# A graph network layer on one core: order of the vector steps, a third PSUM home for gathered rows, and another order at the end

## The chip, the cores and the metric

One core of one Trainium2 chip. The metric is device time of one execution in microseconds (us), median of the runs shown. Engines: TensorE (PE in the profile; PEld its weight loads), VectorE (DVE), ScalarE (ACT), GpSimd (POOL), SyncE (SP, DMA issue only).

## What is computed

Two graph layers over N = 256 nodes with 512 features and E = 4352 edges. The change lies in the second layer; cut to it, the reference is:

```python
hs = xs @ w_in2f_s / sqrt(B);  hv = einsum('nbc,bf->nfc', xv, w_in2f_v) / sqrt(B)   # B = 128, F = 32
s, v = hs[idx_j], hv[idx_j]                   # gather by edge
h = ssp(f_ij @ W1 + b1)                       # ssp(x) = softplus(x) - log 2
Wf = ((h @ W2 + b2) * rcut).reshape(-1, F, 6)
# per edge, with ys = Yr[:, 0], yv = Yr[:, 1:4]: s*ys*Wf0, (v.yv)*Wf1/sqrt 3, s*yv*Wf2, v*ys*Wf3
agg = segment_sum(edge, idx_i, n)             # scatter by edge
s_in = concat(agg[..., 0], agg[..., 1]);  v_in = concat(agg[..., 2:5], agg[..., 5:8])
os1 = ssp(s_in @ w_f2o1_s / sqrt(2F));    os2 = os1 @ w_f2o2_s / sqrt(B)
ov2 = (v_in through w_f2o1_v, then w_f2o2_v, each scaled)
out = x + concat(os2, ov2)
```

## The kernel before

Edges lie on partitions, in 34 tiles of 128, in nine groups of four tiles (the last, group 8 = `LATE`, has two). For each group, counted here by g, the engines do:

- **PE gathers** (`gather`, L721): one-hot columns times the node channels `HL`, whose high and low parts give 128x256 per tile in PSUM; the group's rows live in a pair of PSUM banks, `gpair[g % 2]`, so two groups are in flight. `gather(g)` waits for `MA` of group g - 2, the last step of VectorE that reads that pair.
- **ACT** copies the low parts out (`rows_lo`, L284, semaphore `Glo`), rounds the finished messages to `Mh` (L301 for half 1, released by `svw`; L305 for half 0, released by `MA`), and makes the scatter one-hots `OsR` of the next group (L240). Its order in the iteration of group g is L301(g), L305(g), L240(g + 1), L284(g + 2).
- **VectorE** adds high and low parts (`rows_sum`, L514, semaphore `add`), multiplies by filters times harmonics (`times_w2_y`, L534, `Q`), writes one product to the messages (`times_w1`, L529, `vys`), another (`s_w2_times_y`, L546, `svw`), reduces over three components in place (`sum_of_vy`, L540, `red`), and writes the last product (L565, `MA`). `sum_of_vy` writes over what `times_w1` reads, so it waits for `vys`, then `Q`.
- **POOL** makes the remainders `Ml` = M - Mh of both halves (L395, L399) and scales filters of a later group (L378).
- **PE scatters** (`scatter`, L733): the one-hots against `Mh` and `Ml` into two running aggregates, 0 in bank 4 and 1 in bank 5.

The last groups are scattered in pieces (`scatter_part`, L742), high and low parts apart, as they come; the remainders of group 8 and of half 0 of group 7 are made on VectorE (L572, semaphores `MlA_late`, `MlB_late`). Then aggregate 0 is copied by VectorE (L575) and aggregate 1 by ACT (L313), and two branches follow. The **scalar branch**: L782 (matmul, `os1`), ACT's Abs, Exp and Ln (L315, L317, L319), VectorE's scaled maximum with zero (L577) and the sum of both (L588), L795 (matmul), L591 and the DMA issued by ACT (L321). The **vector branch**: six matmuls (L788 to L790, `fin`), additions of x (L583, L584), and two DMAs on SP's queue (L193). Each engine runs its instructions in the order written here; semaphores are the only other order.

Of the kernel before, what the change touches and what calls it, by code (L numbers as in the profile page):

```python
# [5 lines left out]
def gnn_preln_kernel(nc, x, idx, dst_row, f_t, yr, w0, bias0, w1, w2, b2, w_in, w_o1s, w_o1vt, w_o2s, w_o2v,  # L6
# [8 lines left out]
    P = 128  # L15
# [38 lines left out]
    with ctx:  # L54
# [3 lines left out]
        def sem(name):  # L58
# [74 lines left out]
        ta, te, te2, os1T = (za[:, i * N:(i + 1) * N] for i in range(4))  # L133
# [16 lines left out]
                 "scatA aggA aggT wc wcs o1 os1 ta te tl rl os1T fin os2 ov o")  # L150
# [8 lines left out]
        gpair = (pair[0], pair[3])  # L159
# [7 lines left out]
        def rows_of(g):  # L167

            return gpair[g % 2][:, 0:tiles(g) * 2 * C].rearrange("p (t h c f) -> p t h c f", t=tiles(g), h=2, c=4)
# [27 lines left out]
        def _(act):  # L197
# [114 lines left out]
            act.wait_ge(q["scat"], NG)  # L312
            nc.scalar.activation(aggT[:, 1, :], bank[5][:, 0:N], ACT.Copy).then_inc(q["aggT"], 1)  # L313
# [91 lines left out]
        def _(dve):  # L405
# [113 lines left out]
            for g in range(NG):  # L519
# [55 lines left out]
            nc.vector.tensor_copy(aggT[:, 0, :], bank[4][:, 0:N]).then_inc(q["aggA"], 1)  # L575
            dve.wait_ge(q["ta"], 1)
            nc.vector.tensor_scalar(te2[:], bank[2][:, 0:N], SF, 0.0, ALU.mult, ALU.max).then_inc(q["rl"], 1)  # L577
            for a in range(NH):
                dve.wait_ge(q["fin"], a + 1)
                ov = o_sb[:, a, B:].rearrange("p (d c) -> p c d", c=3)  # L580
                xv = x1[:, a, B:].rearrange("p (d c) -> p c d", c=3)
                xz = bank[a][:, 0:2 * B].rearrange("p (c d) -> p c d", c=2)
                nc.vector.tensor_tensor(ov[:, 0:3:2, :], xz, xv[:, 0:3:2, :], ALU.add)  # L583
                nc.vector.tensor_tensor(ov[:, 1, :], bank[6 + a][:, 0:B], xv[:, 1, :], ALU.add).then_inc(q["ov"], 1)  # L584
                if a == 0:
                    dve.wait_ge(q["tl"], 1)
                    dve.wait_ge(q["rl"], 1)
                    nc.vector.tensor_tensor(os1T[:], te2[:], ta[:], ALU.add).then_inc(q["os1T"], 1)  # L588
# [6 lines left out]
        def _(pe):  # L595
# [109 lines left out]
            def gather(g):  # L705
# [152 lines left out]
```

## Time and profile before

| | us |
|---|---|
| median of 3 runs | 71.74 (71.64 to 71.81) |
| the profiled execution's own time | 71.83 |
| its span, first to last instruction | 69.8 |
| PE, DVE, ACT, POOL busy | 61.7, 60.1, 48.6, 39.5 |
| granted TensorE clock over the span | 0.988 of full |

The span is 2.03 us shorter than the execution's time; what lies around it is not in the trace. The loop over groups takes 34.56 to about 61 us of the span, the rest of the scatter and the two branches take the last nine.

### The profile page before, as it was taken

To read this page: it belongs to the slowest core of one execution; us is meant where nothing else is said; L and a number is where in the kernel's file an instruction comes from. 1 tells how busy PE (TensorE), PEld (TensorE's weight loads), DVE (VectorE), ACT (ScalarE), POOL (GpSimd) and SP (SyncE) were. 2 spreads that over 40 slices of the span, in tenths; PEclk is the share of its full clock that TensorE was granted. 3 is DMA by queue.
4 is the path that set the end of the run, shared out by engine and by line. 5 is a ranking of instruction groups with operands and counts; after the bars stand their busy time and mean duration, and the time that the engine had idled before them with its cause. 6 is when DMAs were issued, how large, how long until landed. Compare 5 with 4: busy or idle time off the path is not lost.

```text
span 69.8 us, 1215 instructions
## 1 busy us (share of the span) xinstructions
PE 61.7 (88%) x407; PEld 48.6 (70%) x407; DVE 60.1 (86%) x124; ACT 48.6 (70%) x74; POOL 39.5 (57%) x46
## 2 busy tenths in 40 slices
PE   3999998999999999897998979999999999998340
PEld 1236754568834268796987969998898989997220
DVE  4599999999979968989999898989898999972760
ACT  0700059978999697967979999988696969732700
POOL 5000030000676989594799979999999988700000
PEclk9999999999999999999999999999999999999995
DMA  0899998984000000000000000000000000000044
GB/s 1 129 396 247 361 499 379 449 317 124 9 0 0 0 0 0 0 0 5 0 0 0 0 0 9 5 0 0 0 0 0 0 0 9 0 0 0 0 148 153
DMA packets 3049, 5.65 MB, mean 81 GB/s; under 512 B 540, under 2 KB 1936, under 8 KB 2916
## 3 DMA queue, kind: packets, MB, share of 16 engines
q1 hardware_dynamic: 2274, 5.14, 21.3%
q10 hardware_dynamic: 770, 0.44, 2.2%
q8 instruction: 3, 0.05, 0.3%
q14 instruction: 2, 0.02, 0.1%
HBM read 5.06 MB, written 0.52 MB: 80 GB/s over the span
## 4 chain that ended last, share of the span: by engine, by line
DVE 45%; PE 20%; issue 14%; ACT 13%; DMA 3%; DVEq 0%; ACTq 0%
ACT OsR L240 8%; DVE WQ L412 7%; DVE Os L412 7%; PE pair L632 5%; ACT w_sb L284 5%; DVE dst_bc L565 4%; PE pair L733 4%; PE pair L742 4%; DVE pair L514 3%; PE pair L674 3%; DMA idx_sb<-idx 3%; PE pair L721 3%; DVE w_sb L485 2%; DVE za L446 2%; DVE hX L449 2%
## 5 line engine op out<-in xcount | busy, mean ns | idle before, releaser
L733 PE MATMUL pair<-OsR,Mh 128*128 128x256 f32 x56 | 13.6, 281 | 0.0
L733 PE MATMUL pair<-OsR,Ml 128*128 128x256 f32 x56 | 13.6, 281 | 0.0
L721 PE MATMUL pair<-HL,OdT 128*128 128x256 f32 x68 | 10.1, 289 | 1.6 <-DVE dst_bc L565 0.7
L395 POOL TENSOR_TENSOR Ml<-dst_bc,Mh 128x512 fp32r<-128x512 f32 x8 | 10.4, 1305 | 1.1 <-ACT Mh L301 1.0
L721 PEld LDWEIGHTS pair<-HL,OdT 128*128 128x128 f32 x68 | 8.6, 188 | 2.8 <-issue 2.8
L733 PEld LDWEIGHTS pair<-OsR,Ml 128*128 128x128 f32 x56 | 10.5, 188 | 0.0
L733 PEld LDWEIGHTS pair<-OsR,Mh 128*128 128x128 f32 x56 | 10.5, 188 | 0.0
L605 PEld LDWEIGHTS pair<-WQ,Os 128*128 128x128 bf16 x68 | 6.8, 104 | 4.0 <-DVE WQ L412 1.8
L605 PE MATMUL pair<-WQ,Os 128*128 128x256 bf16 x68 | 9.4, 297 | 0.2 <-DVE WQ L412 0.2
L399 POOL TENSOR_TENSOR Ml<-dst_bc,Mh 128x512 fp32r<-128x512 f32 x7 | 9.2, 1309 | 0.0
L240 ACT ACTIVATE OsR<-Os 128x1024 fp32r<-128x1024 bf16 (+1 forms) x9 | 9.0, 999 | 0.0
L632 PE MATMUL pair<-w_sb,h1T 128*128 128x512 f32 x16 | 7.7, 601 | 0.3 <-ACT h1T L214 0.3
L305 ACT ACTIVATE Mh<-dst_bc 128x512 fp32r<-128x512 f32 (+1 forms) x9 | 5.5, 609 | 3.1 <-DVE dst_bc L565 3.0
L514 DVE TENSOR_TENSOR pair<-pair,w_sb 128x512 f32<-128x512 f32 (+1 forms) x10 | 6.2, 619 | 1.3 <-ACT w_sb L284 1.2
L358 POOL TENSOR_SCALAR OdT<-dst_bc,iota_c 128x1088 fp32r<-128x1088 int32 x2 | 6.1, 3054 | 1.6 <-DVE OdT L459 1.4
L341 POOL CAST b2p<-b_sb 96x128 bf16<-96x128 f32 x1 | 1.4, 1402 | 8.3 <-issue 8.3
L534 DVE TENSOR_TENSOR pair<-pair,WQ 128x512 f32<-128x512 f32 (+1 forms) x9 | 6.0, 662 | 0.1
L378 POOL TENSOR_TENSOR WQ<-WQ,y 128x256 f32<-128x256 f32 (+1 forms) x9 | 5.8, 652 | 0.1
L207 ACT ACTIVATE za<-pair 128x512 f32<-128x512 f32 (+1 forms) x3 | 1.4, 489 | 6.3 <-PE pair L613 6.3
L284 ACT ACTIVATE w_sb<-pair 128x512 f32<-128x512 f32 (+1 forms) x10 | 5.2, 518 | 0.8 <-PE pair L721 0.7
L412 DVE TENSOR_TENSOR Os<-iota_r,idp 128x512 bf16<-128x512 bf16 (+3 forms) x7 | 5.6, 796 | 0.0
L412 DVE TENSOR_TENSOR WQ<-iota_r,idp 128x512 bf16<-128x512 bf16 (+3 forms) x7 | 5.6, 796 | 0.0
(122 smaller groups left out, 140.2 us busy)
## 6 DMA issues: line engine op xcount, KB each, us to landing
dst_bc<-dst_row SPq DMA_DIRECT2D x1, 2176.0 KB, 12.9
w_sb<-w SPq DMA_DIRECT2D x1, 1024.0 KB, 8.1
x_sb<-x SPq DMA_DIRECT2D x1, 512.0 KB, 4.4
out<-x_sb SPq DMA_DIRECT2D x2, 192.0 KB, 1.9
f_sb<-f_t SPq DMA_DIRECT2D x1, 378.0 KB
b_sb<-bias SPq DMA_DIRECT2D x1, 256.0 KB, 13.1
w_sb<-w ACTq DMA_DIRECT2D x1, 128.0 KB, 4.1
out<-x_sb ACTq DMA_DIRECT2D x1, 128.0 KB, 1.9
```

What stands on the lines that cost most here:

```text
L240: nc.scalar.activation(OsR[:, g % RG, 0:n, :], Os[:, t0:t0 + n, :], ACT.Copy).then_inc(q["OsR"], 1)
L284: nc.scalar.activation(G_lo[:, g % RS, j0:j1, :, :], rows_of(g)[:, j0:j1, 1, :, :], ACT.Copy).then_inc(q["Glo"], 1)
L358: nc.gpsimd.tensor_scalar(OdT[:, 0, c * E // 4:(c + 1) * E // 4], dst_bc[:, c * E // 4:(c + 1) * E // 4], iota_c[:, 0:1], None, ALU.is_equ ...
L395: nc.gpsimd.tensor_tensor(Ml[:, o, 0:n, feats(1)], M[:, o, 0:n, feats(1)], Mh[:, o, 0:n, feats(1)].bitcast(fp32), ALU.subtract).then_inc(q ...
L399: nc.gpsimd.tensor_tensor(Ml[:, o, 0:n, feats(0)], M[:, o, 0:n, feats(0)], Mh[:, o, 0:n, feats(0)].bitcast(fp32), ALU.subtract).then_inc(q ...
L412: last = nc.vector.tensor_tensor(into[:, t0:t1, :].rearrange("p t (h k) -> p t h k", k=2), nodes, of_edge, ALU.is_equal)
L514: nc.vector.tensor_tensor(hi, hi, G_lo[:, g % RS, j0:j1, :, :].rearrange("p t c f -> p t (c f)"), ALU.add).then_inc(q["add"], 1)
L534: nc.vector.tensor_tensor(L, G, wq[:, :, 3:7, :], ALU.mult).then_inc(q["Q"], 1)
L605: last = nc.tensor.matmul(bank[4 + a][:, 0:N], Os[:, t, a * P:(a + 1) * P], Od[:, t, :], start=(t == 0), stop=(t == T - 1))
L632: last = nc.tensor.matmul(bank[a][:, :], h1T[:, a, k, :], w0_sb[:, k, :], start=(k == 0), stop=(k == KD - 1))
L721: last = nc.tensor.matmul(gpair[g % 2][:, j * 2 * C:(j + 1) * 2 * C], OdT[:, a, t * P:(t + 1) * P], HL[:, a, :, :], start=(a == 0), stop=( ...
L733: last = nc.tensor.matmul(bank[4 + b][:, 0:N], part[:, g % RG, j, feats(b)], OsR[:, g % RG, j, :], start=(TG * g + j == 0 and part is Mh), ...
```

## The change

In VectorE's group, `sum_of_vy` comes ahead of `s_w2_times_y` (but not in group 8), and the last product (L565) comes ahead of `rows_sum` of the next group. Group 7's gathered rows get a third pair of PSUM banks (banks 2 and 3, where the filters were, hence the wait for `Wsb`); group 8 takes pair 3, free after group 5. PE gathers group 7 right behind group 6, and group 8 one step later. At the end PE takes the parts of aggregate 0 first; L782's product stands between the last parts of aggregate 1; both aggregates are copied by VectorE; the three products of a vector output lie in one bank, so that one instruction per half adds x; the sum of the scalar branch is not made by VectorE but by two accumulating matmuls, one of `te2`, one of `ta`.

```diff
-        ta, te, te2, os1T = (za[:, i * N:(i + 1) * N] for i in range(4))
+        ta, te, te2 = (za[:, i * N:(i + 1) * N] for i in range(3))
...
-        gpair = (pair[0], pair[3])
+        gpair = [pair[(0, 3)[g % 2]] for g in range(LATE - 1)] + [pair[1], pair[(0, 3)[LATE % 2 ^ 1]]]
...
-            act.wait_ge(q["scat"], NG)
-            nc.scalar.activation(aggT[:, 1, :], bank[5][:, 0:N], ACT.Copy).then_inc(q["aggT"], 1)
             act.wait_ge(q["os1"], 1)
             nc.scalar.activation(ta[:], bank[2][:, 0:N], ACT.Abs, scale=SF).then_inc(q["ta"], 1)
...
                 times_w2_y()
                 times_w1()
-                s_w2_times_y()
-                sum_of_vy()
-                if g + 1 < NG:
-                    rows_sum(g + 1, 0, tiles(g + 1))
+                if g < LATE:
+                    sum_of_vy()
+                    s_w2_times_y()
+                else:
+                    s_w2_times_y()
+                    sum_of_vy()
                 dve.wait_ge(q["red"], g + 1)
                 nc.vector.tensor_tensor(m[:, :, 0:2, :], G[:, :, 0:2, :], wq[:, :, 0:3:2, :],
                                         ALU.mult).then_inc(q["MA"], 1)
+                if g + 1 < NG:
+                    rows_sum(g + 1, 0, tiles(g + 1))
...
+            dve.wait_ge(q["scat"], NG)
+            nc.vector.tensor_copy(aggT[:, 1, :], bank[5][:, 0:N]).then_inc(q["aggT"], 1)
             dve.wait_ge(q["ta"], 1)
             nc.vector.tensor_scalar(te2[:], bank[2][:, 0:N], SF, 0.0, ALU.mult, ALU.max).then_inc(q["rl"], 1)
             for a in range(NH):
                 dve.wait_ge(q["fin"], a + 1)
-                ov = o_sb[:, a, B:].rearrange("p (d c) -> p c d", c=3)
-                xv = x1[:, a, B:].rearrange("p (d c) -> p c d", c=3)
-                xz = bank[a][:, 0:2 * B].rearrange("p (c d) -> p c d", c=2)
-                nc.vector.tensor_tensor(ov[:, 0:3:2, :], xz, xv[:, 0:3:2, :], ALU.add)
-                nc.vector.tensor_tensor(ov[:, 1, :], bank[6 + a][:, 0:B], xv[:, 1, :], ALU.add).then_inc(q["ov"], 1)
-                if a == 0:
-                    dve.wait_ge(q["tl"], 1)
-                    dve.wait_ge(q["rl"], 1)
-                    nc.vector.tensor_tensor(os1T[:], te2[:], ta[:], ALU.add).then_inc(q["os1T"], 1)
+                nc.vector.tensor_tensor(o_sb[:, a, B:].rearrange("p (d c) -> p c d", c=3),
+                                        bank[a][:, 0:3 * B].rearrange("p (c d) -> p c d", c=3),
+                                        x1[:, a, B:].rearrange("p (d c) -> p c d", c=3), ALU.add).then_inc(q["ov"], 1)
...
-                if g >= 2:
-                    pe.wait_ge(q["MA"], g - 1)
+                if g == LATE - 1:
+                    pe.wait_ge(q["Wsb"], NG)
+                elif g >= 2:
+                    pe.wait_ge(q["MA"], g - 1 if g < LATE else LATE - 2)
...
-            for g in range(2, NG):
+            for g in range(2, LATE - 1):
                 gather(g)
+                if g == LATE - 2:
+                    gather(LATE - 1)
                 if g >= 3:
                     scatter(g - 3, 0)
                 scatter(g - 2, 1)
                 if g + 5 < NG:
                     filters(g + 5)
-            scatter(LATE - 2, 0)
+            gather(LATE)
+            for g in range(LATE - 4, LATE - 1):
+                scatter(g, 0)
+                if g + 1 < LATE - 1:
+                    scatter(g + 1, 1)
             pe.wait_ge(q["OsR"], LATE)
+            pe.wait_ge(q["MhA"], LATE)
+            scatter_part(LATE - 1, 0, Mh)
             pe.wait_ge(q["MhB"], LATE)
             scatter_part(LATE - 1, 1, Mh)
-            pe.wait_ge(q["MhA"], LATE)
-            scatter_part(LATE - 1, 0, Mh)
-            pe.wait_ge(q["MlB"], LATE)
-            scatter_part(LATE - 1, 1, Ml)
             pe.wait_ge(q["OsR"], LATE + 1)
             pe.wait_ge(q["MhB"], LATE + 1)
             scatter_part(LATE, 1, Mh)
+            pe.wait_ge(q["MlA_late"], 1)
+            scatter_part(LATE - 1, 0, Ml)
             pe.wait_ge(q["MhA"], LATE + 1)
             scatter_part(LATE, 0, Mh)
-            pe.wait_ge(q["MlA_late"], 1)
-            scatter_part(LATE - 1, 0, Ml)
             pe.wait_ge(q["MlA_late"], 2)
             scatter_part(LATE, 0, Ml).then_inc(q["scatA"], 1)
-            pe.wait_ge(q["MlB_late"], 1)
-            scatter_part(LATE, 1, Ml).then_inc(q["scat"], 2)
+            pe.wait_ge(q["MlB"], LATE)
+            scatter_part(LATE - 1, 1, Ml)
 
             pe.wait_ge(q["aggA"], 1)
             pe.wait_ge(q["o1"], 1)
             nc.tensor.matmul(bank[2][:, 0:N], o1s_sb[:], aggT[0:64, 0, :], start=True, stop=True).then_inc(q["os1"], 1)
+            pe.wait_ge(q["MlB_late"], 1)
+            scatter_part(LATE, 1, Ml).then_inc(q["scat"], 2)
+            pe.wait_ge(q["wcs"], 1)
+            for a in range(NH):
+                nc.tensor.matmul(bank[a][:, 0:B], aggT[64:128, 0, a * P:(a + 1) * P], wc_sb[64:128, :], start=True, stop=True)
             pe.wait_ge(q["aggT"], 1)
-            pe.wait_ge(q["wcs"], 1)
+            for a in range(NH):
+                nc.tensor.matmul(bank[a][:, 2 * B:3 * B], aggT[64:128, 1, a * P:(a + 1) * P], wc_sb[64:128, :], start=True,
+                                 stop=True).then_inc(q["fin2"], 1)
+            for a in range(NH):
+                pe.wait_ge(q["fin2"], a + 1)
+                nc.tensor.matmul(bank[a][:, B:2 * B], aggT[0:64, 1, a * P:(a + 1) * P], wc_sb[0:64, :], start=True,
+                                 stop=True).then_inc(q["fin"], 1)
             pe.wait_ge(d_o2s, 16)
-            for a in range(NH):
-                n = slice(a * P, (a + 1) * P)
-                nc.tensor.matmul(bank[a][:, 0:B], aggT[64:128, 0, n], wc_sb[64:128, :], start=True, stop=True)
-                nc.tensor.matmul(bank[a][:, B:2 * B], aggT[64:128, 1, n], wc_sb[64:128, :], start=True, stop=True)
-                nc.tensor.matmul(bank[6 + a][:, 0:B], aggT[0:64, 1, n], wc_sb[0:64, :], start=True,
-                                 stop=True).then_inc(q["fin"], 1)
-            pe.wait_ge(q["os1T"], 1)
-            for a in range(NH):
-                n = slice(a * P, (a + 1) * P)
-                nc.tensor.matmul(bank[2 + a][:, 0:B], os1T[:, n], o2s_sb[:], start=True, stop=True).then_inc(q["os2"], 1)
+            pe.wait_ge(q["rl"], 1)
+            for a in range(NH):
+                nc.tensor.matmul(bank[2 + a][:, 0:B], te2[:, a * P:(a + 1) * P], o2s_sb[:], start=True, stop=False)
+            pe.wait_ge(q["tl"], 1)
+            for a in range(NH):
+                nc.tensor.matmul(bank[2 + a][:, 0:B], ta[:, a * P:(a + 1) * P], o2s_sb[:], start=False,
+                                 stop=True).then_inc(q["os2"], 1)
```

VectorE, one full group, before (names in brackets are the semaphores it waits for, `s_` ahead of each):

```order
L534 TENSOR_TENSOR pair<-pair,WQ 128x4x128 [waits s_MlA,s_WYp,s_add]
L529 TENSOR_TENSOR dst_bc<-pair,WQ 128x4x3x32
L546 TENSOR_TENSOR dst_bc<-pair,WQ 128x4x3x32 [waits s_Q]
L540 TENSOR_REDUCE pair<-pair 128x4x32 [waits s_Q,s_vys]
L514 TENSOR_TENSOR pair<-pair,w_sb 128x4x128 [waits s_Glo,s_G]
L565 TENSOR_TENSOR dst_bc<-pair,WQ 128x4x64 [waits s_red]
```

and in the changed kernel, whose lines up to 565 are numbered up to two lower:

```order
L532 TENSOR_TENSOR pair<-pair,WQ 128x4x128 [waits s_MlA,s_WYp,s_add]
L527 TENSOR_TENSOR dst_bc<-pair,WQ 128x4x3x32
L538 TENSOR_REDUCE pair<-pair 128x4x32 [waits s_Q,s_vys]
L544 TENSOR_TENSOR dst_bc<-pair,WQ 128x4x3x32 [waits s_Q]
L565 TENSOR_TENSOR dst_bc<-pair,WQ 128x4x64 [waits s_red]
L512 TENSOR_TENSOR pair<-pair,w_sb 128x4x128 [waits s_Glo,s_G]
```

The reduction now stands right behind the product whose end it waits for, and the row sum is the last of the group, right ahead of the next group's first product, which waits for it.

PE, from the middle of the parts of group 8 to the end, before (`b_sb` is `aggT`, `za` holds `ta`, `te2` and, before, `os1T`):

```order
L742 MATMUL pair<-OsR,Ml 128x256 [waits s_MlA_late]
L742 MATMUL pair<-OsR,Ml 128x256
L742 MATMUL pair<-OsR,Ml 128x256 [waits s_MlB_late]
L742 MATMUL pair<-OsR,Ml 128x256
L782 MATMUL pair<-b_sb,o1s_sb 128x256 [waits s_o1,s_aggA]
L788 MATMUL pair<-wc_sb,b_sb 128x128 [waits dma_o2s,s_wcs,s_aggT]
...
L790 MATMUL pair<-wc_sb,b_sb 128x128
L795 MATMUL pair<-o2s_sb,za 128x128 [waits s_os1T]
L795 MATMUL pair<-o2s_sb,za 128x128
```

and in the changed kernel:

```order
L742 MATMUL pair<-OsR,Ml 128x256 [waits s_MlA_late]
L742 MATMUL pair<-OsR,Ml 128x256
L742 MATMUL pair<-OsR,Ml 128x256 [waits s_MlB]
L742 MATMUL pair<-OsR,Ml 128x256 x3
L786 MATMUL pair<-b_sb,o1s_sb 128x256 [waits s_o1,s_aggA]
L742 MATMUL pair<-OsR,Ml 128x256 [waits s_MlB_late]
...
L794 MATMUL pair<-wc_sb,b_sb 128x128 [waits s_aggT]
L794 MATMUL pair<-wc_sb,b_sb 128x128
L798 MATMUL pair<-wc_sb,b_sb 128x128 [waits s_fin2] x2
L803 MATMUL pair<-o2s_sb,za 128x128 [waits s_rl,dma_o2s]
L803 MATMUL pair<-o2s_sb,za 128x128
L806 MATMUL pair<-o2s_sb,za 128x128 [waits s_tl]
```

L782's product moved ahead of the last two parts of aggregate 1, the vector branch has a new wait (`fin2`) between its products, and the scalar branch ends in two pairs of matmuls behind them.

## Rows read from the trace of the kernel before

**Rows 1.** VectorE's timeline, one group (start, length, engine, line)
```profile
53.60 0.69 DVE L534 TENSOR_TENSOR pair<-pair,WQ 128x512 f32<-128x512 f32 x1
54.20 0.55 DVE L529 TENSOR_TENSOR dst_bc<-pair,WQ 128x384 f32<-128x384 f32 x1
54.67 0.55 DVE L546 TENSOR_TENSOR dst_bc<-pair,WQ 128x384 f32<-128x384 f32 x1
55.13 0.56 DVE L540 TENSOR_REDUCE pair<-pair 128x128 f32<-128x384 f32 x1
55.88 0.70 DVE L514 TENSOR_TENSOR pair<-pair,w_sb 128x512 f32<-128x512 f32 x1 [0.20 <-ACT w_sb L284]
56.49 0.41 DVE L565 TENSOR_TENSOR dst_bc<-pair,WQ 128x256 f32<-128x256 f32 x1
56.82 0.69 DVE L534 TENSOR_TENSOR pair<-pair,WQ 128x512 f32<-128x512 f32 x1
```
**Rows 2.** VectorE's timeline, start of group 8, late remainders
```profile
59.56 0.42 DVE L534 TENSOR_TENSOR pair<-pair,WQ 128x256 f32<-128x256 f32 x1
61.02 1.35 DVE L572 TENSOR_TENSOR Ml<-dst_bc,Mh 128x512 fp32r<-128x512 f32 x3
```
**Rows 3.** VectorE's timeline, two steps that wait for the one before
```profile
27.78 0.49 DVE L488 TENSOR_SCALAR h<-w_sb,xsum 128x512 f32<-128x512 f32 x1
28.30 0.69 DVE L492 SCALAR_TENSOR_TENSOR f_sb<-h 128x512 f32<-128x512 f32 x1
...
33.56 0.91 DVE L514 TENSOR_TENSOR pair<-pair,w_sb 128x256 f32<-128x256 f32 x2
34.56 0.70 DVE L534 TENSOR_TENSOR pair<-pair,WQ 128x512 f32<-128x512 f32 x1
```
**Rows 4.** Groups by form, from 56 us on, VectorE (count | busy, mean ns | idle before)
```profile
L572 DVE TENSOR_TENSOR Ml<-dst_bc,Mh 128x512 fp32r<-128x512 f32 x1 | 0.7, 681 | 0.0
```
**Rows 5.** POOL's timeline, two remainders of the same half, one group apart
```profile
47.08 1.29 POOL L395 TENSOR_TENSOR Ml<-dst_bc,Mh 128x512 fp32r<-128x512 f32 x1
...
50.17 1.31 POOL L395 TENSOR_TENSOR Ml<-dst_bc,Mh 128x512 fp32r<-128x512 f32 x1
```
**Rows 6.** Costliest groups, one scatter matmul; PE's timeline, the last eight parts
```profile
L733 PE MATMUL pair<-OsR,Ml 128*128 128x256 f32 x56 | 13.6, 281 | 0.0
...
62.35 1.11 PE L742 MATMUL pair<-OsR,Ml 128*128 128x256 f32 x8
```
**Rows 7.** ACT's timeline, one rounding; then the end
```profile
59.68 0.63 ACT L305 ACTIVATE Mh<-dst_bc 128x512 fp32r<-128x512 f32 x1 [0.37 <-DVE dst_bc L565]
...
64.48 0.38 ACT L315 ACTIVATE za<-pair 128x256 f32<-128x256 f32 x1 [0.60 <-PE pair L782]
...
65.34 0.51 ACT L319 ACTIVATE za<-za,warm 128x256 f32<-128x256 f32 x1
67.43 0.40 ACTq L321 DMA_DIRECT2D out<-x_sb  x1
```
**Rows 8.** VectorE's timeline, the end
```profile
63.26 0.42 DVE L575 COPY b_sb<-pair 128x256 f32<-128x256 f32 x1 [0.89 <-PE pair L742]
...
65.23 0.49 DVE L583 TENSOR_TENSOR x_sb<-pair,w_sb 128x256 f32<-128x256 f32 x1
...
65.88 0.43 DVE L588 TENSOR_TENSOR za<-za 128x256 f32<-128x256 f32 x1
...
66.89 0.52 DVE L591 SCALAR_TENSOR_TENSOR x_sb<-pair,w_sb 128x128 f32<-128x128 f32 x2
```
**Rows 9.** PE's timeline, the end
```profile
63.74 0.48 PE L782 MATMUL pair<-b_sb,o1s_sb 64*128 64x256 f32 x1 [0.29 <-DVE b_sb L575]
...
64.48 0.27 PE L788 MATMUL pair<-wc_sb,b_sb 64*128 64x128 f32 x1
...
64.59 0.27 PE L788 MATMUL pair<-wc_sb,b_sb 64*128 64x128 f32 x1
...
66.36 0.71 PE L795 MATMUL pair<-o2s_sb,za 128*128 128x128 f32 x4 [1.27 <-DVE za L588]
```

More of the change, by code:

```diff
@@ L149, in gnn_preln_kernel @@
                  "G Glo add vys Q svw red MA MhA MhB MlA MlB MlA_late MlB_late scat "
-                 "scatA aggA aggT wc wcs o1 os1 ta te tl rl os1T fin os2 ov o")
+                 "scatA aggA aggT wc wcs o1 os1 ta te tl rl fin2 fin os2 ov o")
         q = {n: sem("s_" + n) for n in names.split()}
@@ L167, in rows_of @@
         def rows_of(g):
-            return gpair[g % 2][:, 0:tiles(g) * 2 * C].rearrange("p (t h c f) -> p t h c f", t=tiles(g), h=2, c=4)
+            return gpair[g][:, 0:tiles(g) * 2 * C].rearrange("p (t h c f) -> p t h c f", t=tiles(g), h=2, c=4)
         def feats(b):
@@ L720, in gather @@
                     for a in range(NH):
-                        last = nc.tensor.matmul(gpair[g % 2][:, j * 2 * C:(j + 1) * 2 * C], OdT[:, a, t * P:(t + 1) * P],
+                        last = nc.tensor.matmul(gpair[g][:, j * 2 * C:(j + 1) * 2 * C], OdT[:, a, t * P:(t + 1) * P],
                                                 HL[:, a, :, :],
```

## The prediction, made before the changed kernel ran

> **What bounds the kernel now.** I read four views in this order: the busy times, which show PE and VectorE both near nine tenths and so settle nothing; the chain of waits; VectorE's timeline of one group; and the timelines of the last nine microseconds on PE, VectorE and ACT.
>
> VectorE's group lasts 3.22 us (53.60 to 56.82) [rows 1]. Its six steps start 0.60, 0.47, 0.46, 0.75, 0.61 and 0.33 apart. Only the 0.75 is long: the reduction is as large as the products beside it, which are followed after 0.47, so 0.28 of it is a wait. The row names who ended it, ACT's copy of the low parts. That copy stands behind the rounding that the last product released, so there is a ring: last product, ACT's rounding, ACT's one-hots, ACT's copy, row sum, last product. VectorE would need 2.94 for itself. In the first group there was no such wait: seven groups took 22.26 (56.82 less 34.56 [rows 3]), which is 0.28 short of 7 x 3.22.
>
> From group 8 on, something else ends last. PE runs the last eight parts without a gap from 62.35 for 1.11 us [rows 6]; a matmul lasts 0.28 there, so they start (1.11 - 0.28) / 7 = 0.119 apart, and the last part of aggregate 0, the sixth of eight, ends at 62.35 + 5 x 0.119 + 0.28 = 63.22. I call this moment T. VectorE's late remainders begin at 61.02 and are ready in time for that [rows 2]. After T everything is one chain: copy at 63.26 [rows 8], matmul at 63.74 [rows 9], Abs at 64.48 and Ln up to 65.34 + 0.51 = 65.85 [rows 7], VectorE's sum at 65.88, matmuls at 66.36, the two last additions at 66.89, DMA issue at 67.43: T + 4.21.
>
> **The new order on VectorE.** What it removes: the wait of 0.28, since the row sum now comes a product later and ACT is released earlier by both. What it adds: two steps that stand right behind the step whose end they wait for. The reduction waits for the product just ahead (`vys`), and the next group's first product waits for the row sum (`add`). Before, a step lay between in both places. A step that waits for nothing starts 0.09 before the end of the one ahead (53.60 + 0.69 against 54.20) [rows 1]. What a step costs that waits for its neighbour, the loop of before does not show; two places outside show it. The step at 28.30 waits for the one that ends at 27.78 + 0.49 = 28.27: 0.03 behind its end, though it also names a second semaphore, long satisfied. The product at 34.56 waits for row sums that end at 33.56 + 0.91 = 34.47: 0.09 behind [rows 3]. The difference that I see is the order of naming: in the first, the semaphore that ends the wait is the first of the list in the code, in the second it is a later one. In the new loop both waits that matter, `vys` and `add`, are named first, except in group 2, where two one-hot waits come ahead of `add`. So I take 0.03 and, once, 0.09; the bounds are -0.09 (as if nothing waited) and +0.09.
>
> The new group: 0.60 + (0.55 + 0.03) + 0.47 + 0.46 + 0.33 + (0.70 + 0.03) = 3.17 us. Group 0 starts at 34.56 [rows 3], group 7 at 56.82, so seven groups took 22.26; now 7 x 3.17 + 0.06 = 22.25. The first group loses 0.23 (it had no wait to lose) and the six others win it back: nothing is left. Group 7 ends with a row sum of half size, about as long as the half product's 0.42 [rows 2]: 0.60 + 0.58 + 0.47 + 0.46 + 0.33 + 0.45 = 2.89 against 59.56 - 56.82 = 2.74, so 0.15 later. Group 8 keeps its order. The first late remainder moves from 61.02 to 61.02 + 0.14 = 61.16.
>
> Who is behind the moved steps: POOL's remainder of half 1 starts later by about the reduction's 0.47 and its wait, but POOL repeats every 50.17 - 47.08 = 3.09 us [rows 5], less than 3.17, and PE needs it a group later. ACT gets `svw` and `MA` close together; its two roundings then run back to back, at no cost to a chain that no longer passes through ACT.
>
> **The third home and PE's order.** PE gathers groups 7 and 8 earlier, the same number of matmuls; each 0.119. That fills PE's waits for `MA`. It is worth something only if PE is late at the end. It is not: the product `MA` of group 7 starts at 56.81 + 2.11 = 58.92; ACT rounds half 1, then half 0, the latter up to about 60.2 (0.63 long, [rows 7], the two about 0.54 apart). PE then has ten matmuls (7 of half 0, 7 of half 1, 8 of half 1), done near 61.45, and the next part waits for VectorE's remainder until 61.16 + 0.68 [rows 4] + 0.06 (copy end 63.68 to matmul 63.74, [rows 8, 9]) = 61.90. PE stands still for 0.4. So the third home costs nothing and earns nothing here; its gain would show only with a quicker VectorE. T becomes 61.90 + 7 x 0.119 + 0.28 = 63.01, 0.21 earlier; this is the gain of taking aggregate 0 first, four parts and two ahead of it fewer.
>
> **The tail, from T.** The copy ends at T + 0.46, the matmul starts at T + 0.52, as before. A pass of 128 columns takes 0.11 (64.48 to 64.59) [rows 9] and every such matmul is two passes; L786 has 256 columns, so it holds PE for 4 x 0.11, up to T + 0.96. Only then do the two last parts of aggregate 1 run: done at T + 0.96 + 0.12 + 0.28 = T + 1.36 (before: T + 0.24). VectorE's copy of it ends 0.46 later, T + 1.82; the products behind it start at T + 1.88, two passes end at T + 2.26 (0.11 + 0.27); the new wait `fin2` adds 0.06, and the third product of half a is there at T + 2.70. VectorE adds x in one step of 384 elements instead of two of 256 and 128: between the 0.55 of a 384-element product and 0.70 of a 512-element one; the 256-element addition needs 0.49 [rows 8]; I take 0.60, followed after 0.51. Two of them from T + 2.74 hold VectorE to T + 3.76. The scalar branch would be ready earlier: it loses the sum (65.85 to 66.36, 0.51), but its matmuls stand behind all products of the vector branch, four passes for `te2` and then `ta`, and give the first half at T + 3.58. So VectorE is last; the two last additions take 0.52, the DMA issue is at T + 4.30 instead of T + 4.21.
>
> **Sum.** -0.21 + 0.09 = -0.12, against 71.83 of the profiled execution 71.71. The median of the runs is 0.09 below that execution, so 71.62; I say 71.65. What a measurement of this kernel can tell from no change is 0.2%, 0.14 us, so this is just inside.
>
> **Page and trace.** By rows 3 a wait for one's neighbour costs 0.12 to 0.18 against no wait. The Trainium skill, "VectorE: DVE Perf Modes", section "The DRAIN you can't avoid", says that every step waits for the pipe to empty anyway and that a semaphore after each of eight copies cost nothing extra. By that rule both new neighbours are free. That is the first rival; rows 1 speak against it, as steps there start before the one ahead has ended.
>
> **Rivals.**
> - *Neighbours cost nothing.* VectorE's group is 2.94; POOL, at 3.09, sets the end. Its half 0 of group 6, 1.25 behind a start at 47.08 + 3 x 3.09 = 56.35, ends at 58.9; PE has 26 matmuls from there: T = 62.2, which is -1.02 + 0.09: 70.8. For: the page. Against: rows 1 and 3. Chance 0.10.
> - *Neighbours cost 0.09 at every group (slower).* The group is 0.60 + 0.64 + 0.47 + 0.46 + 0.33 + 0.79 = 3.29; seven give +0.77, group 7 +0.27, T = 63.91: +0.69 + 0.09, 72.5. It decides from about 0.05: then VectorE's loss outweighs the four parts. For: the row at 34.56 is the very step in question. Against: there the wait was named later. Chance 0.17.
> - *The scalar branch ends last.* If PE and VectorE pass the vector branch more quickly than I add up, the missing sum shows: tail T + 3.7, 71.1. Against: the chain copy, product, `fin2`, product is rows added up. Chance 0.08.
> - Anything else, as a slower tail by passes that no longer run beside each other: 72.0, chance 0.05.
>
> **How the numbers follow.** The forecast has 0.60, with a range of its own of 71.3 to 72.0 (0.01 on each of fifteen neighbour waits is 0.15; 0.2 on the tail). The range that leaves out most of the first rival and little of the slower one: 71.1 to 72.7. Faster: 0.10 + 0.08 + 0.18 of the forecast's own; within 0.2%: 0.28 of it and 0.02; slower: 0.17 + 0.03 and 0.14 of it.
>
> **What will show it.** Right: a group of 3.17 on VectorE, with no wait for ACT ahead of the row sum; the reduction 0.03 behind the end of `times_w1`; PE idle about 0.4 ahead of the low part of group 7; the last addition of x, not the scalar branch, ahead of the last two steps. Wrong: a group of 3.29 or of 3.1 and less; PE without a gap before T; or a DMA issue nearer to T than 4.0.

## The result and the profile after

The changed kernel takes 72.53 us (median; 72.45 to 72.61) against 71.74 before: ratio 1.0103, 95% interval 1.0068 to 1.0137. It is slower by 0.7 to 1.4%, where I had forecast a hair under no change (71.65); 72.53 lies in the range, the sign does not fit the forecast. The profiled execution took 72.53 as well, with a span of 70.5 us, against 71.83 and 69.8: 0.70. Ratios and this range leave out executions that ran longer at a lower granted clock, the medians do not, and of the last experiment, whose profiled execution was one of them, only the end is read (granted clock 1.00 from 38 us on).

The chain that ended last, from the page of the kernel before; then busy times and chain from the page of the changed kernel:

```profile
DVE 45%; PE 20%; issue 14%; ACT 13%; DMA 3%; DVEq 0%; ACTq 0%
```

```profile
PE 62.5 (89%) x411; PEld 49.5 (70%) x411; DVE 60.8 (86%) x122; ACT 48.2 (68%) x73; POOL 40.2 (57%) x46
...
DVE 70%; PE 16%; issue 6%; DMA 3%; DVEq 1%
```

The busy times say nothing, as before. The chain does: ACT, 13% of it before, is gone, and VectorE went from 45% to 70%. The ring through ACT was broken, as the change does by its order. VectorE's timeline shows what took its place: one group, the answer to [rows 1], then the step into group 2.

```profile
53.67 0.70 DVE L532 TENSOR_TENSOR pair<-pair,WQ 128x512 f32<-128x512 f32 x1
54.28 0.55 DVE L527 TENSOR_TENSOR dst_bc<-pair,WQ 128x384 f32<-128x384 f32 x1
54.86 0.57 DVE L538 TENSOR_REDUCE pair<-pair 128x128 f32<-128x384 f32 x1
55.34 0.55 DVE L544 TENSOR_TENSOR dst_bc<-pair,WQ 128x384 f32<-128x384 f32 x1
55.80 0.41 DVE L565 TENSOR_TENSOR dst_bc<-pair,WQ 128x256 f32<-128x256 f32 x1
56.13 0.69 DVE L512 TENSOR_TENSOR pair<-pair,w_sb 128x512 f32<-128x512 f32 x1
56.86 0.70 DVE L532 TENSOR_TENSOR pair<-pair,WQ 128x512 f32<-128x512 f32 x1
```

```profile
40.05 0.69 DVE L512 TENSOR_TENSOR pair<-pair,w_sb 128x512 f32<-128x512 f32 x1
40.94 0.70 DVE L532 TENSOR_TENSOR pair<-pair,WQ 128x512 f32<-128x512 f32 x1 [0.20 <-DVE pair L512]
```

A group lasts 3.19. The reduction starts 0.03 behind the product it waits for (54.28 + 0.55 = 54.83, then 54.86), the next product 0.04 behind the row sum (56.13 + 0.69 = 56.82); neither the reduction nor the row sum waits for ACT. In group 2, where four semaphores are waited for, the gap is 0.20.

The end on VectorE (compare [rows 2, 8]), PE (compare [rows 6, 9]) and ACT (compare [rows 7]):

```profile
59.77 0.43 DVE L532 TENSOR_TENSOR pair<-pair,WQ 128x256 f32<-128x256 f32 x1
...
61.24 1.35 DVE L574 TENSOR_TENSOR Ml<-dst_bc,Mh 128x512 fp32r<-128x512 f32 x3
63.22 0.42 DVE L577 COPY b_sb<-pair 128x256 f32<-128x256 f32 x1 [0.63 <-PE pair L742]
64.86 0.42 DVE L579 COPY b_sb<-pair 128x256 f32<-128x256 f32 x1 [1.22 <-PE pair L742]
...
66.41 1.27 DVE L584 TENSOR_TENSOR x_sb<-pair,w_sb 128x384 f32<-128x384 f32 x2 [0.79 <-PE pair L798]
67.59 0.48 DVE L589 SCALAR_TENSOR_TENSOR x_sb<-pair,w_sb 128x128 f32<-128x128 f32 x2
```

```profile
60.40 1.42 PE L742 MATMUL pair<-OsR,Mh 128*128 128x256 f32 x10
61.98 0.73 PE L742 MATMUL pair<-OsR,Ml 128*128 128x256 f32 x4 [0.16 <-DVE Ml L574]
62.55 0.39 PE L742 MATMUL pair<-OsR,Mh 128*128 128x256 f32 x2
62.78 0.88 PE L742 MATMUL pair<-OsR,Ml 128*128 128x256 f32 x6
63.70 0.70 PE L786 MATMUL pair<-b_sb,o1s_sb 64*128 64x256 f32 x2
64.33 0.50 PE L742 MATMUL pair<-OsR,Ml 128*128 128x256 f32 x2
64.76 0.71 PE L791 MATMUL pair<-wc_sb,b_sb 64*128 64x128 f32 x4
65.34 0.71 PE L794 MATMUL pair<-wc_sb,b_sb 64*128 64x128 f32 x4
65.89 0.71 PE L798 MATMUL pair<-wc_sb,b_sb 64*128 64x128 f32 x4
```

```profile
64.44 0.38 ACT L313 ACTIVATE za<-pair 128x256 f32<-128x256 f32 x1 [2.66 <-PE pair L786]
...
68.11 0.40 ACTq L319 DMA_DIRECT2D out<-x_sb  x1
```

The last part of aggregate 0 is the second of the six at 62.78: T = 62.78 + 0.12 + 0.28 = 63.18. Two stretches tell the rest, and I use them for every kernel below: the loop, from the start of group 0's product to the copy of aggregate 0, and the end, from that copy to the DMA issue. What lies ahead of group 0 is not touched by the change and varies by 0.4 between profiled executions, so start times alone would mislead. Before: 34.56, 63.26, 67.43 [rows 3, 7, 8], so 28.70 and 4.17. After: 34.40, 63.22, 68.11, so 28.82 and 4.89. The loop costs 0.12, the end 0.72; together 0.84, of which the earlier start hides 0.16 in this pair of traces.

### The profile page after: what moved, and what is told of

It reads as the page before. It is cut to its first block, busy times and chain, and to the rows that moved or that the text cites. A ratio compares the mean times of both kernels' runs of the same rounds, so it can differ in the third digit from the quotient of the medians.

```text
span 70.5 us, 1219 instructions
## 1 busy us (share of the span) xinstructions
PE 62.5 (89%) x411; PEld 49.5 (70%) x411; DVE 60.8 (86%) x122; ACT 48.2 (68%) x73; POOL 40.2 (57%) x46
## 4 chain that ended last, share of the span: by engine, by line
DVE 70%; PE 16%; issue 6%; DMA 3%; DVEq 1%
DVE pair L532 9%; DVE pair L512 8%; DVE WQ L410 8%; DVE Os L410 7%; DVE pair L538 7%; DVE dst_bc L527 5%; PE pair L630 5%; DVE dst_bc L565 5%; PE pair L672 3%; DMA idx_sb<-idx 3%; PE pair L742 2%; DVE w_sb L483 2%; DVE za L444 2%; DVE hX L447 2%; DVE x_sb L584 2%
## 5 line engine op out<-in xcount | busy, mean ns | idle before, releaser
L603 PE MATMUL pair<-WQ,Os 128*128 128x256 bf16 x68 | 8.4, 276 | 1.2 <-DVE WQ L410 1.2
L333 POOL TENSOR_TENSOR y<-yr_sb 128x136 f32<-128x136 f32 x1 | 1.3, 1278 | 8.0 <-DMA yr_sb<-yr 8.0
```

Of the source, the lines that this page charges most:

```text
L603: last = nc.tensor.matmul(bank[4 + a][:, 0:N], Os[:, t, a * P:(a + 1) * P], Od[:, t, :], start=(t == 0), stop=(t == T - 1))
```

## The experiments

All against runs of the kernel before on the same chip. The first four tell loop from end, and in each one candidate.

**The loop alone**, the kernel before with the new order on VectorE, the third home and the early gathers, and its own order of parts and its own end:

```diff
+                if g < LATE:
+                    sum_of_vy()
+                    s_w2_times_y()
...
+                if g + 1 < NG:
+                    rows_sum(g + 1, 0, tiles(g + 1))
...
+        gpair = [pair[(0, 3)[g % 2]] for g in range(LATE - 1)] + [pair[1], pair[(0, 3)[LATE % 2 ^ 1]]]
```

> The kernel before with the changed loop alone (VectorE's order, third home, PE's gathers ahead), and with the old order of parts and the old tail. Theory A (the tail lost the time, the loop is even): VectorE's group 3.18, last part of aggregate 0 ends within 0.15 us of where it ended before, DMA issue 4.2 us behind it, 71.7 to 71.9 us. Theory B (the neighbour waits of the loop lost it): 72.3 us or more.

**The parts and the end alone**, the other half of the diff on the loop of before:

```diff
+            dve.wait_ge(q["scat"], NG)
+            nc.vector.tensor_copy(aggT[:, 1, :], bank[5][:, 0:N]).then_inc(q["aggT"], 1)
...
+            pe.wait_ge(q["MlB_late"], 1)
+            scatter_part(LATE, 1, Ml).then_inc(q["scat"], 2)
```

> The kernel before with the new order of parts and the new tail alone, old loop. Theory A: the last part of aggregate 0 ends near 62.9 to 63.1 (four parts fewer ahead of it, and VectorE's remainders at 61.0 no longer early enough to hide), the DMA issue stands 4.9 behind it as in the changed kernel, so 72.2 to 72.4 us. Theory B: 71.6 us or less.

**Parts first**, the changed kernel with the last two parts of aggregate 1 ahead of the scalar branch's product:

```diff
+            pe.wait_ge(q["MlB_late"], 1)
+            scatter_part(LATE, 1, Ml).then_inc(q["scat"], 2)
             pe.wait_ge(q["aggA"], 1)
             pe.wait_ge(q["o1"], 1)
             nc.tensor.matmul(bank[2][:, 0:N], o1s_sb[:], aggT[0:64, 0, :], start=True, stop=True).then_inc(q["os1"], 1)
-            pe.wait_ge(q["MlB_late"], 1)
-            scatter_part(LATE, 1, Ml).then_inc(q["scat"], 2)
```

> The changed kernel with the two last parts of aggregate 1 ahead of the product of the scalar branch (L786) instead of behind it. Theory A with the place named (the vector branch is behind because its aggregate waits for L786 on PE): its copy is over about 1 us earlier, the additions of x begin about 0.45 earlier, held then by PE's passes, 72.0 to 72.2 us. Rival (the two extra waits of fin2 and the 384-element additions carry all of it): 72.5 us, no change.

**The naming**, the changed kernel with two waits of a product exchanged:

```diff
-                dve.wait_ge(q["add"], g + 2)
                 dve.wait_ge(q["WYp"], g + 1)
+                dve.wait_ge(q["add"], g + 2)
```

> The changed kernel, in the loop's first product the wait for the row sum named second, behind the wait for POOL's scaling, instead of first. If the place in the list sets the price: 0.09 instead of 0.03 behind the row sum in seven groups, a group of 3.24, 0.4 us in all, 72.9 to 73.0 us. If it does not: 72.5 us.

Measured (in brackets the ratio to the kernel before and its 95% interval): the loop alone 72.03 us (1.0051, 1.0005 to 1.0098), the end alone 72.24 (1.0078, 1.0055 to 1.01), parts first 71.73 (1.0, 0.9964 to 1.0037), the naming 72.97 (1.0184, 1.011 to 1.0258). The median of the loop alone stands for little: seven of its twelve runs took 71.66 to 72.17, five 72.56 to 72.71. In the traces the loop alone has 28.75 + 4.17, the end alone 28.46 + 4.88. So the whole loss at the end is there without the new loop, and moving one matmul takes more than all of it away: parts first has 28.82 + 3.97, where I had expected 72.0 us or more. The two halves of the change do not add up to it: +0.05 and +0.47 in the traces, against 0.84. Of the 0.32 that are missing, 0.31 lie ahead of the copy of aggregate 0: with the old loop the new order of parts brings it forward (28.70 to 28.46), with the new loop it does not (28.75 to 28.82).

VectorE's and PE's timelines of parts first:

```profile
63.54 0.43 DVE L577 COPY b_sb<-pair 128x256 f32<-128x256 f32 x1 [0.63 <-PE pair L742]
64.25 0.42 DVE L579 COPY b_sb<-pair 128x256 f32<-128x256 f32 x1 [0.28 <-PE pair L742]
```

```profile
63.10 1.11 PE L742 MATMUL pair<-OsR,Ml 128*128 128x256 f32 x8
64.15 0.48 PE L789 MATMUL pair<-b_sb,o1s_sb 64*128 64x256 f32 x1
64.15 0.49 PE L792 MATMUL pair<-wc_sb,b_sb 64*128 64x128 f32 x2
64.47 0.38 PE L789 MATMUL pair<-b_sb,o1s_sb 64*128 64x256 f32 x1
64.48 0.38 PE L792 MATMUL pair<-wc_sb,b_sb 64*128 64x128 f32 x2
```

The second copy starts 0.71 behind the first, where it was 1.64; and the scalar branch's product (L789, rows 0 to 63 of the aggregate) now runs beside the first product of the vector branch (L792, rows 64 to 127) instead of alone.

The naming, on VectorE's timeline at the step from one group to the next:

```profile
46.69 0.69 DVE L512 TENSOR_TENSOR pair<-pair,w_sb 128x512 f32<-128x512 f32 x1
47.47 0.70 DVE L532 TENSOR_TENSOR pair<-pair,WQ 128x512 f32<-128x512 f32 x1
```

0.09 behind the row sum's end (47.38) instead of 0.03, a group of 3.24, and a loop of 29.17, 0.35 longer than the change's. The time is 0.44 above the changed kernel's. What is waited for is the same, only the place in the list differs.

**Three parts of the change alone**, each on the kernel before: the new order on VectorE; the third home with the early gathers; and the scalar sum as accumulating matmuls.

```diff
+                if g < LATE:
+                    sum_of_vy()
+                    s_w2_times_y()
...
+                if g + 1 < NG:
+                    rows_sum(g + 1, 0, tiles(g + 1))
```

> The kernel before with VectorE's order alone. Theory A (the neighbour waits give back what the ring took): groups of 3.18 in place of 3.22, the first 0.25 longer, group 2 longer by 0.16; last part of aggregate 0 at the same place within 0.15 us, 71.7 to 71.9 us. Rival (PE's gathers ahead are what keeps the changed loop even): 72.1 us or more.

```diff
+        gpair = [pair[(0, 3)[g % 2]] for g in range(LATE - 1)] + [pair[1], pair[(0, 3)[LATE % 2 ^ 1]]]
...
+            gather(LATE)
+            for g in range(LATE - 4, LATE - 1):
+                scatter(g, 0)
```

> The kernel before with the third home and PE's gathers ahead alone. In the old loop PE runs without a gap up to the last parts, so matmuls pulled into its earlier waits shorten the end: last part of aggregate 0 about 0.35 us earlier, 71.4 to 71.5 us. Rival (the gathers ahead only move the wait): 71.8 us.

```diff
-                    nc.vector.tensor_tensor(os1T[:], te2[:], ta[:], ALU.add).then_inc(q["os1T"], 1)
...
+                nc.tensor.matmul(bank[2 + a][:, 0:B], te2[:, a * P:(a + 1) * P], o2s_sb[:], start=True, stop=False)
...
+                nc.tensor.matmul(bank[2 + a][:, 0:B], ta[:, a * P:(a + 1) * P], o2s_sb[:], start=False,
+                                 stop=True).then_inc(q["os2"], 1)
```

> The kernel before with the scalar branch's sum left to two accumulating pairs of matmuls, all else old. Theory A: without fin2 and without the passes in a row, VectorE's additions end 0.36 us earlier (the sum's place on VectorE) and the last two follow at once, 71.4 to 71.5 us. Rival (the pairs of matmuls stand behind one another and cost what the sum did): 71.8 us.

The order alone: 71.89 (1.003, 1.0007 to 1.0054), 28.76 + 4.17. The home alone: 72.2 (0.998, 0.9958 to 1.0002; profiled 71.32), 28.37 + 4.17. The scalar sum in matmuls: 71.36 (0.9956, 0.9943 to 0.997), 28.69 + 3.76. So the third home with the early gathers is worth 0.33 in the trace of the old loop (the interval of its runs reaches 1.0002, so they alone can't tell it from nothing), and nothing in the new one (28.76 without, 28.75 with). The scalar sum is worth 0.41 at the end.

Why the home earns nothing in the new loop, the last scatter of group 6 shows: it waits for `MlA`, POOL's remainder. First the kernel before, then the home alone, then the loop alone; each time PE's first matmul of that scatter, and in the last two POOL's remainder ahead of it:

```profile
59.51 0.28 PE L733 MATMUL pair<-OsR,Mh 128*128 128x256 f32 x1
```

```profile
57.51 1.30 POOL L399 TENSOR_TENSOR Ml<-dst_bc,Mh 128x512 fp32r<-128x512 f32 x1
...
58.95 0.36 PE L735 MATMUL pair<-OsR,Mh 128*128 128x256 f32 x1
```

```profile
58.09 1.30 POOL L399 TENSOR_TENSOR Ml<-dst_bc,Mh 128x512 fp32r<-128x512 f32 x1
...
59.53 0.36 PE L739 MATMUL pair<-OsR,Mh 128*128 128x256 f32 x1
```

Before, POOL was done at 58.96 and PE, which had run without a gap since 57.61, came only 0.55 later. The home takes that slack away: PE starts 0.14 behind POOL's end (58.81). In the new loop the remainder ends 24.77 behind group 0's start instead of 24.40, and PE starts 0.14 behind it with the home (59.53) and 0.15 without (59.52). From there the parts run without a gap, so gathers taken earlier only lengthen the wait for POOL.

**The old vector branch** on parts first: the third product back in its own bank, no `fin2`, two additions per half:

```diff
-                                        bank[a][:, 0:3 * B].rearrange("p (c d) -> p c d", c=3),
+                nc.vector.tensor_tensor(ov[:, 0:3:2, :], xz, xv[:, 0:3:2, :], ALU.add)
+                nc.vector.tensor_tensor(ov[:, 1, :], bank[6 + a][:, 0:B], xv[:, 1, :], ALU.add).then_inc(q["ov"], 1)
```

> The changed kernel with the parts of aggregate 1 ahead of the scalar branch's product (as in e3) and the old vector branch: third product in a bank of its own, no fin2, two additions per half. If fin2 and the shared bank cost by holding the two kinds of product one behind the other: the additions begin about 0.3 us earlier against e3, and 71.4 to 71.5 us. If not: as e3, 71.7 us.

71.64 (1.0011, 0.9973 to 1.0048), 28.82 + 3.90: the shared bank, `fin2` and the long additions cost 0.07 of the end there, which the runs can't tell from nothing. Its copies and its DMA issue, for the last experiment below:

```profile
63.27 0.42 DVE L577 COPY b_sb<-pair 128x256 f32<-128x256 f32 x1 [0.64 <-PE pair L744]
63.98 0.42 DVE L579 COPY b_sb<-pair 128x256 f32<-128x256 f32 x1 [0.29 <-PE pair L744]
...
67.17 0.41 ACTq L319 DMA_DIRECT2D out<-x_sb  x1
```

**ACT's order**, the kernel before with the one-hots of the next group ahead of the rounding of half 0. It breaks the same ring without touching VectorE:

```diff
+                if g + 1 < NG:
+                    scatter_onehots(g + 1)
                 act.wait_ge(q["MA"], g + 1)
                 nc.scalar.activation(Mh[:, o, 0:n, feats(0)], M[:, o, 0:n, feats(0)], ACT.Copy).then_inc(q["MhA"], 1)
-                if g + 1 < NG:
-                    scatter_onehots(g + 1)
```

> The kernel before with one thing changed: ACT makes the next group's one-hots ahead of the rounding of half 0, in the time in which it waited for the last product. This shortens the ring without a neighbour wait on VectorE. If the ring is what sets 3.22: groups of about 3.07 (the copy then waits for PE's gather, 0.16 less), the loop 0.9 us shorter, but PE without a gap near the end gives back part: 71.2 us. If POOL at 3.09 or PE sets the pace: 71.6 us.

71.16 (0.9928, 0.9904 to 0.9951), 28.19 + 4.17. VectorE's timeline, then ACT's:

```profile
54.49 0.56 DVE L540 TENSOR_REDUCE pair<-pair 128x128 f32<-128x384 f32 x1
55.12 0.70 DVE L514 TENSOR_TENSOR pair<-pair,w_sb 128x512 f32<-128x512 f32 x1
```

```profile
54.42 0.60 ACT L284 ACTIVATE w_sb<-pair 128x512 f32<-128x512 f32 x1 [0.51 <-PE pair L721]
```

The row sum follows the reduction's start after 0.63 instead of 0.75, and ACT's copy waits 0.51 for PE's gather where before it waited for nothing. The group is 3.10 (52.96 to 56.06). The loop is 0.51 shorter, not the 0.9 that I had expected.

**The good parts together**: the kernel before with aggregate 0's parts first, all parts ahead of the scalar branch's product, and the scalar sum in matmuls; then the same with ACT's order:

```diff
-            pe.wait_ge(q["MlB"], LATE)
-            scatter_part(LATE - 1, 1, Ml)
...
+            pe.wait_ge(q["MlB"], LATE)
+            scatter_part(LATE - 1, 1, Ml)
...
+                nc.tensor.matmul(bank[2 + a][:, 0:B], te2[:, a * P:(a + 1) * P], o2s_sb[:], start=True, stop=False)
```

> The kernel before with aggregate 0's parts first (all parts ahead of the scalar branch's product) and the scalar branch's sum left to the matmuls; old loop, old vector branch, aggregate 1 copied by ACT. Sum of what the traces show: last part of aggregate 0 0.24 us earlier, 0.36 from the sum, 71.2 us.

> e10 together with ACT's order of e9. The parts first need an early VectorE to pay and the ring's cut gives it: about 1.0 us before the last part of aggregate 0, 0.36 behind it, 70.5 us. If PE's work is the floor: 71.0 us.

71.26 (0.9929, 0.9915 to 0.9943), 28.46 + 3.90; with ACT's order 70.81 (0.9865, 0.9828 to 0.9902), 27.73 + 3.89. The second beats both kernels, the one before by 1.0 to 1.7%; the gains of its two halves add (0.9928 x 0.9929 = 0.9858). Of the first, the end is 0.14 longer than with the scalar sum in matmuls alone (3.76): with aggregate 0 first, the copy of aggregate 1 starts 0.71 behind that of aggregate 0 (63.64 against 62.93), where it was 0.23 before (63.49 against 63.26). So of the 0.24 that this order gives ahead of the copy 0.10 is left, by the traces; the intervals of the two kernels' runs touch. The second kernel's copy and DMA issue:

```profile
62.21 0.42 DVE L575 COPY b_sb<-pair 128x256 f32<-128x256 f32 x1 [0.64 <-PE pair L738]
...
66.10 0.40 ACTq L321 DMA_DIRECT2D out<-x_sb  x1
```

**The product between the parts**, the first of those two kernels with the product put where the change puts it, and nothing else of the new vector branch:

```diff
-            nc.scalar.activation(aggT[:, 1, :], bank[5][:, 0:N], ACT.Copy).then_inc(q["aggT"], 1)
+            nc.vector.tensor_copy(aggT[:, 1, :], bank[5][:, 0:N]).then_inc(q["aggT"], 1)
...
-            pe.wait_ge(q["MlB_late"], 1)
-            scatter_part(LATE, 1, Ml).then_inc(q["scat"], 2)
             nc.tensor.matmul(bank[2][:, 0:N], o1s_sb[:], aggT[0:64, 0, :], start=True, stop=True).then_inc(q["os1"], 1)
+            pe.wait_ge(q["MlB_late"], 1)
+            scatter_part(LATE, 1, Ml).then_inc(q["scat"], 2)
```

> The kernel e10 (old loop, aggregate 0's parts first, both copies and all parts ahead of the scalar branch's product, old vector branch; 71.26 us, copy of aggregate 0 to the last DMA issue 3.90 us) with one thing moved: the scalar branch's product of 64 rows (two passes) stands between the two parts of aggregate 0 and the last two parts of aggregate 1, and VectorE copies aggregate 1 behind aggregate 0. No shared bank and no split addition here. Theory 1, the product's place alone costs: it waits for the copy of aggregate 0, so that the last two parts and the copy behind them start some 0.9 us later; copy to DMA issue 4.6 to 4.8 us, 72.0 to 72.1 us. Theory 2, the place costs only together with the shared bank and split addition: copy to DMA issue 3.9 to 4.1 us, 71.3 to 71.5 us.

72.06 (1.0051, 1.0031 to 1.0072): 0.80 above its twin. Its copies and its DMA issue:

```profile
64.88 0.42 DVE L573 COPY b_sb<-pair 128x256 f32<-128x256 f32 x1 [0.63 <-PE pair L738]
66.52 0.42 DVE L575 COPY b_sb<-pair 128x256 f32<-128x256 f32 x1 [1.22 <-PE pair L738]
...
69.61 0.40 ACTq L319 DMA_DIRECT2D out<-x_sb  x1
```

The copies are 1.64 apart, as in the changed kernel, and the end lasts 4.73 instead of 3.90. Against its twin it also has the copy of aggregate 1 on VectorE instead of ACT. That is not what costs: the kernel with the old vector branch on parts first has both copies on VectorE as well, its end (63.27 to 67.17) is 3.90 too, and from its end to this one only the product's place differs. So the place costs 0.83 with the old vector branch, and 0.92 with the new one (4.89 against 3.97). What remains between this kernel and the changed one, 4.89 less 4.73, is the new vector branch: 0.16, from one trace each.

All of them together. Ratios are to the kernel before on the same chip; loop and end are from the profiled execution:

| kernel | expected (first theory), us | median us | ratio | loop + end |
|---|---|---|---|---|
| before | | 71.74 | | 28.70 + 4.17 |
| changed | 71.65 | 72.53 | 1.0103 | 28.82 + 4.89 |
| loop alone | 71.7 to 71.9 | 72.03 | 1.0051 | 28.75 + 4.17 |
| end alone | 72.2 to 72.4 | 72.24 | 1.0078 | 28.46 + 4.88 |
| parts first | 72.0 to 72.2 | 71.73 | 1.0 | 28.82 + 3.97 |
| naming | 72.9 to 73.0 | 72.97 | 1.0184 | 29.17 + 4.89 |
| order alone | 71.7 to 71.9 | 71.89 | 1.003 | 28.76 + 4.17 |
| home alone | 71.4 to 71.5 | 72.2 | 0.998 | 28.37 + 4.17 |
| scalar sum in matmuls | 71.4 to 71.5 | 71.36 | 0.9956 | 28.69 + 3.76 |
| old vector branch on parts first | 71.4 to 71.5 | 71.64 | 1.0011 | 28.82 + 3.90 |
| ACT's order | 71.2 | 71.16 | 0.9928 | 28.19 + 4.17 |
| good parts | 71.2 | 71.26 | 0.9929 | 28.46 + 3.90 |
| good parts and ACT's order | 70.5 | 70.81 | 0.9865 | 27.73 + 3.89 |
| product between the parts | 72.0 to 72.1 | 72.06 | 1.0051 | not read, 4.73 |

## Why the prediction was wrong

**The loop, right in kind, a little low.** The ring, the two neighbour waits and their price were right: a group of 3.18 to 3.19 against 3.17, the reduction 0.03 behind its neighbour. The choice of 0.03 over 0.09 by the order of naming was the step with most at stake, and exchanging two names shows that it holds. Seven groups took 56.86 - 34.40 = 22.46 against 22.25. Of the 0.21, 0.12 is group 1 with the step into group 2 (40.94 - 37.59 = 3.35 against 3.23): I took a gap of 0.09, and it is 0.20; the rest is 0.01 to 0.02 a group. Group 7 took 2.91 (2.89), the first remainder came 1.47 behind group 8's start (1.46), and the matmul that waits for it 0.74 behind that (0.74). Then PE's eight matmuls up to T took 63.18 - 61.98 = 1.20 against 1.11: the four after the wait are 0.57 from the next, not 4 x 0.119 = 0.48. One step of the loop's sum was wrong without deciding the time: "PE needs it a group later", said of POOL's remainder. In the last groups PE needs it at once: it starts the last scatter of group 6 at 59.31, 0.15 behind POOL's end (57.88 + 1.28), and VectorE's later remainder then hides that. In all T is 28.78 behind group 0's start, where 63.01 - 34.56 = 28.45 was forecast: 0.33 of the miss, and the loop's -0.21 became +0.12.

**"The gain of taking aggregate 0 first"** exists: with the old loop it is 28.70 to 28.46, 0.24, of which the end gives 0.14 back. In the new loop it is gone, for the reason that the prediction had half seen: PE stands still ahead of group 7's low part (0.16 by the row at 61.98, from the end of the ten matmuls at 61.82; counted as I did, from 0.12 behind the start of the last of them, it is free at 61.66 instead of 61.45 and stands for 0.32 instead of 0.4), and VectorE decides when T comes. Its late remainders start 61.24 - 34.40 = 26.84 behind group 0, where it was 61.02 - 34.56 = 26.46 [rows 2, 3]; the part order can't shorten that.

**"The third home costs nothing and earns nothing here"** holds in the new loop (28.75 against 28.76). Its reason, that PE is not late at the end, was wrong for the old loop, where the home is worth 0.33: there PE was the last, by 0.55 behind POOL. In the new loop with the old order of parts it is POOL's remainder that takes the gain, in the changed kernel that and VectorE's late remainder.

**The tail is the step that failed**: "the DMA issue is at T + 4.30 instead of T + 4.21". It was at T + 4.93. Point by point:
- The copy of aggregate 1 over at T + 1.82: it was over at 65.28, T + 2.10. "L786 has 256 columns, so it holds PE for 4 x 0.11": it held it from 63.70 to 64.33, 0.63, and the two parts behind it took 0.50, not 0.40. The trace of the kernel before had the price: its two passes start at 63.74 and 64.06, 0.32 apart, and the 0.11 was read off products of 128 columns. The second pass there:

```profile
64.06 0.38 PE L782 MATMUL pair<-b_sb,o1s_sb 64*128 64x256 f32 x1
```

- The third product at VectorE at T + 2.74: at 66.41, T + 3.23, another 0.21. Four passes behind each other take 0.55 (65.34 to 65.89), not 0.44, and from the first pass of the third product to VectorE's addition it is 0.52 (65.89 to 66.41), not 0.42. The additions' own row names PE as what they waited for.
- Two additions of 384 elements in 1.02: they took 67.59 - 66.41 = 1.18.
- The two last additions and the issue, 0.54: 0.52.

These are 0.28 + 0.21 + 0.16 - 0.02 = 0.63. With the loop's 0.33 they are the whole miss of 0.96 between -0.12 and the 0.84 of the traces. I had priced PE's work by the spacing of matmuls that follow each other without a wait; the places here are behind a wait or at a change between products of 64 and of 128 rows. That this is why they last longer fits the rows, but no run tests it. The mechanism, that the parts and with them the copy come later, was in the sum, but its price stood only in the net, T + 3.76 for the vector branch; what all parts first would give was never added up beside it. The kernels with the old vector branch put that price at 0.83, and the changed kernel against parts first at 4.89 - 3.97 = 0.92. By my own sum the scalar branch was not the last, so its early product bought nothing.

**The rivals.** The time of the second, 72.5, came true but not its mechanism: no group was 3.29. The small last one, "a slower tail by passes that no longer run beside each other", at 0.05 and 72.0, has the slower tail right, larger than I put it, but its reason only in part: the scalar branch's product does run alone now, but in the last experiment the vector branch's passes do run beside each other, on two halves of rows, and the end still lasts 4.73:

```profile
67.00 0.37 PE L784 MATMUL pair<-wc_sb,b_sb 64*128 64x128 f32 x1 [0.52 <-DVE b_sb L575]
67.02 0.37 PE L786 MATMUL pair<-wc_sb,b_sb 64*128 64x128 f32 x1
```

Neighbours that cost nothing are refuted: 0.03 behind the end, against 0.09 ahead of it for a step that waits for nothing [rows 1], is 0.12 each, twice per group. What the Trainium skill, "VectorE: DVE Perf Modes", section "The DRAIN you can't avoid", states, that a semaphore after each of eight copies cost nothing extra, does not hold for these steps. The rival's 70.8 was never near. The scalar branch did not end last: ACT was done with its part at 65.30 + 0.51, VectorE's additions began only at 66.41, and the two last additions follow them without a wait (67.59).

**Still open.** What the 0.63 of the 64-row product is made of: 0.32 are from its first pass to its second, in parts first as in the kernel before; the rest was not measured by itself. Why group 2 has a gap of 0.20 with two satisfied waits named ahead of the one that counts, but 0.13 in the naming experiment with three, was not tried. And the loop alone reads +0.05 in its trace, but +0.04 to +0.70 by its interval; which is nearer is not settled.

## What to carry to other kernels

Where work that waits for a fresh result is put in front of work whose inputs are ready, on an engine that runs its instructions in order, the wait is paid by everything behind it: here one short product ahead of the last two parts cost 0.83 us. To break a ring of waits, try first to move the step on the engine that has slack (here ACT's order: 0.9928 of the time) rather than on the one that sets the pace (VectorE's order: 1.003), since neighbours there pay for each semaphore between them, 0.12 each here; and a gain ahead of a wait that another edit makes the last one is lost. Price a matmul behind a wait from a row behind a wait, and a product of 256 columns from one of 256 columns; the kernel before has such a row at 63.74.

## What the runs showed of the hardware

- Of several waits of one VectorE step, the place of the one that counts sets the gap behind its end: 0.03 named first, 0.09 named second (the group 3.18 against 3.24), 0.20 in group 2 with two one-hot waits ahead, but 0.13 with three ahead in the naming experiment, cause open.
- PE's first matmuls behind a wait are slower at a granted clock of 1.0: four took 0.57 instead of 0.48. Most of it is the first: in the changed kernel the second matmul follows after 0.19 or 0.20 (58.07 to 58.26, 59.31 to 59.51), elsewhere in a row after 0.12.
- A product of 64 rows and 256 columns in fp32 held PE for 0.63 when a product of 128 rows followed (0.32 from its first pass to its second), and ran beside a product on the other 64 rows (both at 64.15) when one was ready.
